# Another order on all five engines, and other PSUM banks, in a kernel of two cross-attention blocks

## The chip, the cores and the metric
The kernel runs on one core of a Trainium2 chip. The metric is the device time in microseconds (us) of one execution. Three runs of the kernel before took 1828.81, 1827.54 and 1826.35 us, median 1827.54.

## The reference, cut to what matters
x and ctx are 64 batches x 128 tokens x 256 features, float32. Two blocks follow one another; ctx is the source of keys and values in both.

```python
def block0(q, ctx):                       # 16 heads x 64
    qh, kh, vh = ln(q) @ Wq, ln(ctx) @ Wk, ln(ctx) @ Wv
    p = softmax((qh @ kh.T + rel_bias[i - j + 511]) / 8)
    x = q + (p @ vh) @ fc_w.T + fc_b
    h = ln(x)
    return x + gelu(h @ W1.T + b1) @ W2.T + b2        # 256 -> 1024 -> 256

def block1(x, ctx):                       # 16 query heads x 16, one kv head
    q, k, v = x @ Wq + bq, ctx @ Wk + bk, ctx @ Wv + bv
    p = softmax(where(window, q @ k.T / 4, -1e9))
    a = (p @ v) @ Wo + bo
    g = silu(concat(a, x) @ Wg + bg)
    o = a * g + x * (1 - g)
    y = o * rsqrt(mean(o * o) + 1e-6) * rms_w
    return y - mean(y, axis=tokens)
```

## The kernel before, in words
Two batches make a group (`GROUP = 2`), so there are `NG` = 32 groups of 256 tokens. Heads are worked on in quads: group g has four quads Q of four heads in block 0, and in block 1 two batches b of 16 heads. A number is kept as a high part (HI) and the rest (LO), and every large product is three matmuls, LO x HI, HI x LO and HI x HI: `mm3` (L616 to L618), or, where the low part comes from VectorE later than the high part from ScalarE, as two parts, `moving_hi` (L622, L623) and `moving_lo` (L626), or `standing_hi` (L630, L631) and `standing_lo` (L634). Operations that end in `_lo` are the second parts.

TensorE's operations, with the tiles into which they divide the array:
- full array, "weight-stationary": `proj_q`, `proj_k` (12 matmuls of 256 columns for one quad), `mlp_in`, `proj_q1`. The weights are the stationary operand and the tokens stream (a row names them as out<-moving,stationary: `bank<-xT,wq`). "Token-stationary" are `proj_v`, `fc`, `mlp_out`, `out_mm`, where the operands have exchanged roles (`wv,cT`, `wfc,OT`, `w,hidS`, `wog,o1T`).
- full array, others: `turn_h`, `turn_x2` (transposes, L640), `center_out` (L965, L967), which subtracts the mean over tokens.
- 64 rows: `scores(g, Q)` (L790), 16 matmuls in pairs that run side by side in the two halves of the array, into two banks.
- 64 columns: `pv(g, Q)` (L803), probabilities times values.
- 32 rows: `scores1(g, b)` (L915), 16 matmuls into four banks. 32 columns: `pv1(g, b, n)` (L928) and `kv` (L702).

The other engines empty the banks and work on what is in them. VectorE (DVE): `k_out` (L1626), `min0` and `min1` (bias or window added and row minimum, L1646, L1754), `inv`, `turn0`/`turn1` (32x32 transposes, L239), the low parts `o_lo` (L1672), `hid_lo` (L1717), layer-norm statistics. ScalarE (ACT): `exps0` and `exps1` (L2520, L2600), `q_out`, `v_out`, `hid_out`, `gelu`, the high parts `hid_hi` (L2571), `o1_hi` (L2613), `x_hat_hi` (L2636). GpSimd (POOL): `norm0`, `norm1` (L3049, L3058; probabilities times the reciprocal of their sum), the gate and residual arithmetic. SyncE (SP) issues the DMAs: `spread0`, `spread1` put the transposed probabilities where pv and pv1 read them, `keys_in` loads block 1's keys, `in_x`, `raw_x`, `out_x` and the like move activations.

Each engine has a program of its own, in an order that is written out by hand: a prologue, a loop `for r in range(3, NG - 3)` of 26 rounds (SP L519, PE L1118, DVE L2045, ACT L2764, POOL L3245), and a tail for the last groups. An engine does its list strictly in that order. A round r works on several groups at once: scores(r, ...) for group r, fc and mlp for r-1, block 1 for r-2 and r-3, proj_q(r + 1, 0) ahead. Order among engines is by semaphores that count events: `till.wait_ge("k_out", 4 * g + Q + 1)` waits until that many `k_out` were done, and the tuples in the calls, such as `("min1", 8 * r - 15)`, name the event that made the PSUM bank free (`freed`, L196). There are 8 PSUM banks; some are taken in turns through `ring_a`, `ring_c`, `ring_d`. `keep_busy` (L643) issues small matmuls that nobody reads, at four places where TensorE waits in prologue and tail.

TensorE's round before, where | is a change of tile shape (17 in a round, the last one to the next round's pv):

```
pv(r-1,2) | fc(r-1,1) k(r,0) k_lo(r,0) fc_lo(r-1,1) q(r,1) k(r,1) fc(r-1,2) | scores(r,0) | pv(r-1,3) |
scores(r,1) | fc(r-1,3) fc_lo(r-1,2) q(r,2) k(r,2) v(r,0) fc_lo(r-1,3) | scores1(r-2,1) | pv1 kv pv1 |
q(r,3) center_out(r-3,1) k(r,3) out_mm(r-2,0) out_mm_lo | pv(r,0) | scores(r,2) | turn_h v(r,1) mlp_in 0
mlp_in_lo mlp_in 1 v(r,2) mlp_in 2 fc(r,0) q(r+1,0) mlp_in 3 mlp_out(0,0) fc_lo(r,0) mlp_out(0,1)
mlp_out_lo(0,0) | pv(r,1) | scores(r,3) | pv1 pv1 | mlp_out_lo(0,1) mlp_out(1,0) center_out(r-2,0)
mlp_out(1,1) mlp_out_lo(1,0) mlp_out_lo(1,1) out_mm(r-2,1) turn_x2 q_lo(r+1) out_mm_lo q1(r-1) q1_lo
v(r,3) | scores1(r-1,0) |
```

## Time and profile before

| | before |
|---|---|
| runs | 1828.81, 1827.54, 1826.35 us |
| the profiled execution's own time | 1826.95 us |
| its span, first to last instruction | 1825.2 us |
| granted TensorE clock, mean | 0.997 of full |
| PE, PEld busy | 1792.8, 1650.3 us |
| DVE, ACT, POOL busy | 1485.3, 1535.3, 1292.3 us |

PE is TensorE's matmuls, PEld its weight loads, which lie beside them. "Busy" joins overlapping instructions; a share is of the span. Matmuls are pipelined: one is listed with 0.28 us and the next starts 0.11 us later, so distances from start to start are what adds up.

### The profile page before, as it was taken

The page shows a single profiled execution, that of the slowest core. Times are in us where ns is not written, and L with a number is a line of the kernel's source. Part 1 is how long each engine was busy: PE and PEld are TensorE (multiplying, and loading weights), DVE is VectorE, ACT ScalarE, POOL GpSimd, SP SyncE. Part 2 cuts the span into 40 slices and gives each one's busy share as a digit, 9 for nine tenths or more (in the row PEclk, how much of TensorE's full clock was granted, in tenths as well). Part 3 has the DMA queues.
Part 4 walks back from the last instruction along what each step waited for, and adds up shares of the span by engine and source line. Part 5 has one row for each costly group of instructions (what it writes and reads, how often), then busy time and mean ns, then how long its engine had stood idle before and what let it go on. Part 6 is the DMA issues. An engine that isn't in the chain of part 4 may idle for free.

```text
span 1825.2 us, 55273 instructions
## 1 busy us (share of the span) xinstructions
PE 1792.8 (98%) x18702; PEld 1650.3 (90%) x18702; DVE 1485.3 (81%) x6755; ACT 1535.3 (84%) x5586; POOL 1292.3 (71%) x1324
## 2 busy tenths in 40 slices
...
GB/s 235 124 95 116 126 122 127 122 113 114 128 118 131 121 113 114 126 119 131 121 114 114 123 121 128 121 118 112 123 124 124 121 121 112 119 118 122 103 89 59
DMA packets 238059, 219.11 MB, mean 120 GB/s; under 512 B 48848, under 2 KB 220240, under 8 KB 237776
## 3 DMA queue, kind: packets, MB, share of 16 engines
...
q14 instruction: 134, 1.10, 0.2%
...
## 4 chain that ended last, share of the span: by engine, by line
PE 90%; DVE 4%; ACT 2%; POOL 1%; DMA 1%; issue 1%; SPq 0%; POOLq 0%; DVEq 0%; ACTq 0%
PE bank L616 11%; PE bank L618 11%; PE bank L617 11%; PE bank L630 9%; PE bank L634 8%; PE bank L631 8%; PE bank L790 7%; PE bank L803 7%; PE bank L915 4%; PE bank L928 3%; PE bank L626 3%; PE bank L622 3%; PE bank L623 3%; PE bank L640 2%; DVE soft L1754 1%
## 5 line engine op out<-in xcount | busy, mean ns | idle before, releaser
L2600 ACT ACTIVATE soft<-soft,row_min 128x128 f32<-128x128 f32 x1024 | 397.3, 392 | 60.9 <-DVE row_min L1754 60.8
L2520 ACT ACTIVATE soft<-soft,row_min 128x128 f32<-128x128 f32 x1024 | 398.5, 393 | 17.1 <-DVE row_min L1646 16.6
L3049 POOL TENSOR_TENSOR soft<-soft,inv_sum 128x512 f32<-128x512 f32 x256 | 271.4, 1061 | 145.7 <-DVE inv_sum L1654 145.7
L239 DVE STREAM_TRANSPOSE turned<-soft 128x512 f32<-128x512 f32 x512 | 341.8, 689 | 10.8 <-POOL soft L3058 4.7
L3058 POOL TENSOR_TENSOR soft<-soft,inv_sum 128x512 f32<-128x512 f32 x256 | 263.9, 1042 | 60.8 <-DVE inv_sum L1763 60.7
L1754 DVE CUSTOM_DVE_ANT_0 soft<-bank,winb 128x128 f32<-128x128 f32 x1024 | 230.3, 283 | 39.0 <-PE bank L915 36.3
L1646 DVE CUSTOM_DVE_ANT_0 soft<-bank,relb 128x128 f32<-128x128 f32 x1024 | 230.0, 281 | 15.3 <-PE bank L803 5.5
L2600 ACT ACTIVATION_READ_ACCUMULATOR soft<-soft,row_min 128x1 f32 x1024 | 195.2, 191 | 0.0
L2520 ACT ACTIVATION_READ_ACCUMULATOR soft<-soft,row_min 128x1 f32 x1024 | 195.0, 190 | 0.0
L790 PE MATMUL bank<-kT,qT 64*128 64x128 f32 x2048 | 148.7, 285 | 0.7 <-DVE kT L1626 0.7
L616 PE MATMUL bank<-wv,cT 128*128 128x256 f32 x512 | 146.5, 286 | 0.0
L790 PEld LDWEIGHTS bank<-kT,qT 64*128 64x128 f32 x2048 | 124.3, 187 | 22.3 <-issue 17.2
L617 PE MATMUL bank<-wv,cT 128*128 128x256 f32 x512 | 143.4, 280 | 0.0
L618 PE MATMUL bank<-wv,cT 128*128 128x256 f32 x512 | 143.3, 280 | 0.0
L803 PE MATMUL bank<-soft,V 128*64 128x128 f32 x2048 | 140.0, 279 | 1.4 <-DMA soft<-turned 0.9
L1717 DVE TENSOR_TENSOR hidS<-hid,hidS 128x1024 fp32r<-128x1024 f32 x64 | 86.8, 1356 | 64.5 <-ACT hidS L2571 63.2
L803 PEld LDWEIGHTS bank<-soft,V 128*64 128x64 f32 x2048 | 109.2, 136 | 30.0 <-issue 19.8
L630 PE MATMUL bank<-wfc,OT 128*128 128x256 f32 x512 | 130.5, 290 | 0.0
L630 PE MATMUL bank<-w,hidS 128*128 128x256 f32 x512 | 128.0, 285 | 0.4 <-ACT hidS L2571 0.3
L631 PE MATMUL bank<-w,hidS 128*128 128x256 f32 x512 | 124.8, 278 | 0.0
L631 PE MATMUL bank<-wfc,OT 128*128 128x256 f32 x512 | 124.0, 278 | 0.0
L2552 ACT ACTIVATE hid<-bank,cols 128x256 f32<-128x256 f32 x256 | 102.3, 468 | 10.4 <-DVE hidS L1717 10.2
...
## 6 DMA issues: line engine op xcount, KB each, us to landing
soft<-turned SPq DMA_DIRECT2D x1024, 128.0 KB, 2.7
...
```

Source lines behind the costliest of these rows:

```text
L239: return eng.transpose(turned[:, slot, :, s % 2, :, :].rearrange("p j h b -> p h j b"), soft[:, s, :, :].rearrange("p h (j a) -> p h j a", ...
L616: pe.matmul(out, stat(LO), mov(HI), start=first, stop=False, **kw)
L617: pe.matmul(out, stat(HI), mov(LO), start=False, stop=False, **kw)
L618: return pe.matmul(out, stat(HI), mov(HI), start=False, stop=last, **kw)
L630: pe.matmul(out, stat(HI), mov(LO), start=first, stop=False, skip_group_check=True)
L631: return pe.matmul(out, stat(HI), mov(HI), start=False, stop=False, skip_group_check=True)
L790: last = pe.matmul(bank[i][:, h * SEQ:(h + 1) * SEQ], qT[half, Q % NQ_BUF, c, b * SEQ:(b + 1) * SEQ], kT[half, Q % NQ_BUF, c, b * SEQ:(b + ...
L803: last = pe.matmul(bank[row:row + HS, col:col + SEQ], V[:, Q % NQ_BUF, b, c * P + row:c * P + row + HS], pair_of_slots(Q % 2)[:, :, slot, ...
L2520: last = act.activation(soft[:, s, h, :], soft[:, s, h, :], ACT.Exp, bias=row_min[:, s, h:h + 1], scale=-1.0, accum_out=row_sum[:, s, h:h ...
L2600: last = act.activation(soft[:, s, h, :], soft[:, s, h, :], ACT.Exp, bias=row_min[:, s, h:h + 1], scale=-1.0, accum_out=row_sum[:, s, h:h ...
L3049: pool.tensor_tensor(soft[:, m % NS0, :, :], soft[:, m % NS0, :, :], inv_sum[:, m % NS0, :].unsqueeze(2).broadcast_to([P, QUAD, SEQ]), ALU ...
L3058: pool.tensor_tensor(soft[:, s, :, :], soft[:, s, :, :], inv_sum[:, s, :].unsqueeze(2).broadcast_to([P, QUAD, SEQ]), ALU.mult).then_inc(se ...
```

## The change
Only orders, banks and the waits that go with them are changed; the operations, their number and their inner code are the same on every engine. The rings become `ring_a` = banks (5, 6), `ring_b` = (3, 1), `ring_c` = (0, 2), and banks 4 and 7 are named alone. TensorE's round is now (15 changes of tile shape):

```
pv(r-1,2) | fc(r-1,1) v(r,0) fc_lo(r-1,1) fc(r-1,2) k(r,0) k_lo(r,0) q(r,1) k(r,1) fc_lo(r-1,2) |
scores(r,0) scores(r,1) | pv(r-1,3) | v(r,1) fc(r-1,3) fc_lo(r-1,3) q(r,2) q(r,3) | scores1(r-2,1) |
pv1 pv1 kv | k(r,2) center_out(r-3,1) k(r,3) turn_h | pv(r,0) | scores(r,2) scores(r,3) | out_mm(r-2,0)
out_mm_lo mlp_in 0 mlp_in_lo mlp_in 1 mlp_in 2 mlp_in 3 fc(r,0) q(r+1,0) v(r,2) mlp_out(0,0)
mlp_out_lo(0,0) mlp_out(0,1) mlp_out_lo(0,1) | pv(r,1) | pv1 pv1 | mlp_out(1,0) center_out(r-2,0)
mlp_out(1,1) mlp_out_lo(1,0) mlp_out_lo(1,1) out_mm(r-2,1) turn_x2 q_lo(r+1) out_mm_lo q1(r-1)
fc_lo(r,0) q1_lo v(r,3) | scores1(r-1,0) |
```

In the tail the changes of tile shape go from 82 to 72, and `keep_busy` has 7, 23, 47, 6 and 28 matmuls at five places where it had 7, 22, 44 and 12 at four. In the prologue only waits and banks at its end differ. Some waits are added that hold in round 3 only. VectorE's list puts `turn1(r-1, 0, 1)` directly ahead of `k_out(r, 1)` and three of `o_lo` at other places; GpSimd's keeps `times_z` and `minus_x` ahead of `norm1(r-2, 0, 0)` and `(0, 1)` and moves `times_gate` behind them. The diff, cut to its core:

```diff
-        ring_a = [banks[i] for i in (0, 5)]
-        ring_c = [banks[i] for i in (2, 7, 3)]
-        ring_d = [banks[i] for i in (4, 6)]
+        ring_a = [banks[i] for i in (5, 6)]
+        ring_b = [banks[i] for i in (3, 1)]
+        ring_c = [banks[i] for i in (0, 2)]
...
@@ SP, the loop
                 spread1(r - 2, 0, 1)
+                spread0(r, 0)
                 out_x(r + 1)
-                spread0(r, 0)
+                in_x(r + 1)
                 raw_x(r + 1)
-                in_x(r + 1)
                 store(r - 3, 1)
-                keys_in(r - 1)
+                tokens_c(r + 1)
                 spread0(r, 1)
-                tokens_c(r + 1)
                 spread1(r - 2, 1, 0)
                 spread1(r - 2, 1, 1)
                 out_c(r + 1)
+                in_c(r + 1)
+                keys_in(r - 1)
                 raw_c(r + 1)
-                in_c(r + 1)
+                store(r - 2, 0)
                 spread0(r, 2)
-                store(r - 2, 0)
...
@@ PE, the loop
-                proj_k(r, 1, ring_c[(r + 1) % 3], ("min1", 8 * r - 14))
-                fc(r - 1, 2, ring_a[(r + 1) % 2])
-                scores(r, 0, (ring_c[r % 3], ring_d[(r + 1) % 2]), (("min1", 8 * r - 13),), (("min1", 8 * r - 12),))
-                pv(r - 1, 3, ring_a[r % 2], ("k_out", 4 * r + 1))
-                scores(r, 1, (ring_d[r % 2], ring_c[(r + 2) % 3]), (("o_lo", 4 * r - 1),), (("v_out", 4 * r),))
...
+                proj_k(r, 1, banks[7], ("min1", 8 * r - 13))
+                fc_lo(r - 1, 2, ring_c[(r + 1) % 2])
+                if r == 3:
+                    till.wait_ge("min1", 12)
+                scores(r, 0, (banks[4], ring_a[r % 2]), (("min1", 8 * r - 12),), (("o_lo", 4 * r - 1),))
+                scores(r, 1, (ring_b[r % 2], ring_c[r % 2]), (("k_out", 4 * r + 1),), (("q_out", 4 * r + 2),))
...
+                pv(r - 1, 3, ring_b[(r + 1) % 2], ("v_out", 4 * r))
+                proj_v(r, 1, ring_a[(r + 1) % 2], ("v_out", 4 * r + 1))
+                fc(r - 1, 3, ring_c[(r + 1) % 2])
...
+                scores(r, 2, (ring_b[(r + 1) % 2], banks[4]), (("min1", 8 * r - 9),), (("y_out", 2 * r - 4),))
+                scores(r, 3, (banks[7], ring_a[r % 2]), (("k_out", 4 * r + 3),), (("k_out", 4 * r + 4),))
+                out_mm(r - 2, 0, ring_c[r % 2], ("min1", 8 * r - 8))
...
@@ ACT, the loop
                 gelu(r - 1, 1)
+                hid_hi(r - 1, 1)
                 x_hat_hi(r - 2, 0)
-                hid_hi(r - 1, 1)
+                v_out(r, 2, ring_b[(r + 1) % 2])
+                o1_hi(r - 2, 1, banks[4])
                 exps0(r, 6)
-                o1_hi(r - 2, 1, banks[1])
...
```

## Rows read from the trace of the kernel before

**Rows 1.** The page: busy us, share, instructions; shares of the last chain.
```profile
PE 1792.8 (98%) x18702; PEld 1650.3 (90%) x18702; DVE 1485.3 (81%) x6755; ACT 1535.3 (84%) x5586; POOL 1292.3 (71%) x1324
...
PE 90%; DVE 4%; ACT 2%; POOL 1%; DMA 1%; issue 1%; SPq 0%; POOLq 0%; DVEq 0%; ACTq 0%
```

**Rows 2.** One round: stretch, us, busy PE PEld DVE ACT POOL, PEclk, DMA, GB/s.
```profile
873.37:927.95 54.58, 54.56 (x580) 50.49 (x576) 45.49 (x210) 47.36 (x175) 40.32 (x42) 1.00 0.48 120
```

**Rows 3.** PE's waits from 160 to 1620 us: total, times, longest.
```profile
PE bank L790 <- DVE kT L1626: 0.7, 2, 0.5
PE bank L630 <- ACT hidS L2571: 0.3, 1, 0.3
```

**Rows 4.** Timeline of PE (start, us): scores(17, 0), pv(16, 3), scores(17, 1).
```profile
935.70 1.16 PE L790 MATMUL bank<-kT,qT 64*128 64x128 f32 x16
936.79 1.09 PE L803 MATMUL bank<-soft,V 128*64 128x128 f32 x16
937.81 0.38 PE L790 MATMUL bank<-kT,qT 64*128 64x128 f32 x2
```

**Rows 5.** Timeline of PE inside scores(17, 0): two narrow windows.
```profile
935.91 0.50 PE L790 MATMUL bank<-kT,qT 64*128 64x128 f32 x6
...
936.25 0.50 PE L790 MATMUL bank<-kT,qT 64*128 64x128 f32 x6
```

**Rows 6.** Timeline of PE: proj_k(16, 2), proj_v(16, 0), proj_q(17, 3).
```profile
887.15 0.28 PE L616 MATMUL bank<-cT,wk 128*128 128x256 f32 x1
...
888.51 0.28 PE L616 MATMUL bank<-wv,cT 128*128 128x256 f32 x1
...
888.98 0.28 PE L617 MATMUL bank<-wv,cT 128*128 128x256 f32 x1
...
947.38 0.38 PE L616 MATMUL bank<-xT,wq 128*128 128x256 f32 x1
947.61 0.28 PE L617 MATMUL bank<-xT,wq 128*128 128x256 f32 x1
...
948.78 0.28 PE L618 MATMUL bank<-xT,wq 128*128 128x256 f32 x1
```

**Rows 7.** Timeline of PE: mlp_out(15, 1, 0), out_mm(14, 1).
```profile
916.85 0.74 PE L634 MATMUL bank<-w,hidS 128*128 128x256 f32 x4
917.60 0.38 PE L630 MATMUL bank<-w,hidS 128*128 128x256 f32 x1
917.82 0.28 PE L631 MATMUL bank<-w,hidS 128*128 128x256 f32 x1
...
919.79 1.10 PE L634 MATMUL bank<-w,hidS 128*128 128x256 f32 x8
920.91 0.47 PE L630 MATMUL bank<-wog,o1T 128*128 128x512 f32 x1
921.22 0.40 PE L631 MATMUL bank<-wog,o1T 128*128 128x512 f32 x1
```

**Rows 8.** Timeline of ACT: x_hat_hi, hid_hi, o1_hi (in brackets: idle before, releaser).
```profile
916.19 0.41 ACT L2636 CAST o1T<-ag 128x256 fp32r<-128x256 f32 x1 [1.42 <-DVE ag L1810]
916.50 1.04 ACT L2571 CAST hidS<-hid 128x1024 fp32r<-128x1024 f32 x1
...
920.41 0.35 ACT L2613 CAST o1T<-bank 128x256 fp32r<-128x256 f32 x1
```

**Rows 9.** Timelines: PE scores1; DVE k_out, o_lo, k_out; POOL norm1.
```profile
926.88 1.15 PE L915 MATMUL bank<-kpar,q1T 32*128 32x256 f32 x16
...
932.59 0.84 DVE L1626 TENSOR_SCALAR kT<-bank,bk 128x256 f32<-128x256 f32 x2
...
934.57 0.65 DVE L1672 TENSOR_TENSOR OT<-bank,OT 128x512 fp32r<-128x512 f32 x1
...
935.95 0.84 DVE L1626 TENSOR_SCALAR kT<-bank,bk 128x256 f32<-128x256 f32 x2
...
932.75 1.04 POOL L3058 TENSOR_TENSOR soft<-soft,inv_sum 128x512 f32<-128x512 f32 x1 [0.35 <-DVE inv_sum L1763]
```

More of the change, by code:

```diff
@@ new lines, in tensor_program @@
+                fc(r - 1, 3, ring_c[(r + 1) % 2])
+                fc_lo(r - 1, 3, ring_c[(r + 1) % 2])
+                proj_q(r, 2, banks[7], ("k_out", 4 * r + 2))
+                proj_q(r, 3, banks[4], ("min0", 8 * r + 1))
+                scores1(r - 2, 1, (ring_a[r % 2], ring_b[r % 2], ring_b[(r + 1) % 2], ring_c[r % 2]), (("min0", 8 * r + 2),), (("min0", 8 * r + 3),), (("o_lo", 4 * r),), (("min0", 8 * r + 4),))
+                pv1(r - 2, 0, 0, ring_a[(r + 1) % 2], ("v_out", 4 * r + 2))
@@ L1350, in tensor_program @@
-            scores(NG - 1, 3, (banks[6], banks[5]), (("o_lo", 4 * NG - 3),), (("hid_out", 4 * NG - 6),))
-            mlp_in(NG - 2, 3, banks[2], ("v_out", 4 * NG - 2))
-            mlp_out(NG - 2, 0, 0, banks[7], ("k_out", 4 * NG))
+            pv1(NG - 5, 0, 1, banks[2])
+            proj_v(NG - 3, 2, banks[7], ("v_out", 4 * NG - 10))
+            center_out(NG - 6, 1, banks[4], ("min1", 8 * NG - 35))
+            proj_q(NG - 3, 2, banks[6], ("min1", 8 * NG - 34))
+            proj_q(NG - 3, 3, banks[5], ("min1", 8 * NG - 33))
@@ new lines, in tensor_program @@
+            proj_k(NG - 3, 3, banks[0], ("min0", 8 * NG - 18))
+            mlp_in(NG - 4, 2, banks[4], ("y_out", 2 * NG - 10))
+            mlp_in(NG - 4, 3, banks[5], ("ag", 2 * NG - 9))
+            scores(NG - 3, 3, (banks[2], banks[3]), (("hid_out", 4 * NG - 15),), (("hid_out", 4 * NG - 14),))
+            pv(NG - 3, 1, banks[0], ("k_out", 4 * NG - 8))
+            mlp_out(NG - 4, 0, 0, banks[6], ("o_lo", 4 * NG - 11))
+            mlp_out_lo(NG - 4, 0, 0, banks[6])
+            fc(NG - 3, 0, banks[4], ("hid_out", 4 * NG - 13))
@@ new lines, in tensor_program @@
+            pv1(NG - 4, 0, 0, banks[1], ("v_out", 4 * NG - 7))
+            pv1(NG - 4, 0, 1, banks[1])
+            kv(NG - 2, banks[2], ("o_lo", 4 * NG - 8))
+            center_out(NG - 5, 1, banks[5], ("k_out", 4 * NG - 5))
+            proj_q(NG - 2, 3, banks[4], ("x1", NG - 2))
+            out_mm(NG - 4, 0, banks[6], ("min1", 8 * NG - 27))
+            proj_v(NG - 2, 1, banks[1], ("o1_lo", 2 * NG - 7))
+            out_mm_lo(NG - 4, 0, banks[6])
+            turn_h(NG - 3, banks[0], ("min1", 8 * NG - 26))
```

1402 lines of the change are left out of this document (684 added, 718 removed).

## The prediction
> **What bounds the kernel now.** I read the page first, by engine and by chain: TensorE (PE) is busy for 1792.8 us of the 1825.2 us span and holds 90% of the chain that ended last; the other engines are busy for 71 to 84% [rows 1]. One round of the loop, from pv(r-1, 2) to the next, takes 54.58 us; PE is busy in 54.56 of them at the full granted clock (1.00) [rows 2]. From 160 to 1620 us the view of waits knows only two things that PE waited for, 1.0 us in all [rows 3]. So PE is bound by its own stream, and only what makes that stream shorter, or tears a hole in it, counts. The other four engines count where PE's cover over them gets thin.
>
> A round has some 576 matmuls, and the change neither adds nor removes one. So I took a round apart by the distance from start to start: (1) what a change of tile shape costs, (2) how far apart two like matmuls start, (3) short waits too small for the view of waits. The sum below is made against the profiled execution (1826.95 us, span 1825.2), 0.6 below the median 1827.54; at the end 0.6 is added.
>
> **1. Tile changes, 17 to 15 a round.** scores(r, 0) takes 936.79 - 935.70 = 1.09 us, from its start to that of the next block [rows 4]. It is eight pairs of matmuls, and inside such a block three pairs take 936.25 - 935.91 = 0.34 us, 0.113 a pair [rows 5]. Eight pairs are 0.91, so 0.18 us is what going into 64-row tiles and out again costs. The change puts scores(r, 0) and scores(r, 1) side by side, and scores(r, 2) and scores(r, 3): two such costs fall away, -0.37 us a round. Nothing else on PE lies beside this, it is start to start. Two of the blocks that remain now have a full-array product behind them in another place, and turn_h (128-column transposes, a cheaper start) no longer opens a stretch; for such differences I add 0.02. **-0.35 a round**, bounds -0.30 and -0.40.
>
> **2. Spacing of full-array matmuls.** The same three products start 0.113 us apart in one place and 0.118 in another. proj_k(r, 2) in the stretch that fc opens: 888.51 - 887.15 = 1.36 us for 12, 0.1133 each; from there proj_v (the operand roles exchanged) takes 0.47 for 4, 0.1175 [rows 6]. proj_q(r, 3), the first after pv1, pays 0.23 for its first step (0.11 extra, the cost of the change) and then 948.78 - 947.61 = 1.17 for 10, 0.117 [rows 6]. Reading all rounds' stretches so: after a tile change, a stretch that begins with a token-stationary product (fc, proj_v) settles to 0.113 and the weight-stationary ones behind it keep that; one that begins weight-stationary stays at 0.117 to 0.118; a step from weight- to token-stationary falls back. About half of the some 350 such distances of a round are long, 0.0046 each, 0.8 us. The new order puts proj_v(r, 1) and fc(r-1, 3) ahead of proj_q(r, 2) and (r, 3) and takes proj_v(r, 0) up behind fc(r-1, 1); but proj_k(r, 2), behind kv, still opens a stretch and out_mm opens one with mlp_in and all of mlp_in's 48 matmuls behind it. Counting so, 125 to 175 stay long, which is 0.58 to 0.80 in place of 0.81. I take **-0.12**; bounds: nearly all short -0.5, all long +0.8.
>
> The row shows two distances. The Trainium skill ("TensorE: Matmul & The Clock Gate", section "Back-to-back issue gap") gives the isolated gap at full clock as N/2.4 + 2.5 ns whatever stands before, 109 ns for 256 columns; by that the order cannot matter, this term is zero and the whole forecast 3 us higher.
>
> **3. Short waits.** Two per round. (a) mlp_out(r-1, 1, 0) needs hid_hi(r-1, 1) of ScalarE. mlp_out_lo's four matmuls ahead of it take 917.60 - 916.85 = 0.75, where 4 x 0.118 and 0.11 for the tile change are 0.58; then its first step takes 0.22 in place of 0.113: 0.17 + 0.11 = 0.28 [rows 7]. On ScalarE x_hat_hi stood ahead of hid_hi and waited 1.42 for VectorE; hid_hi ended at 917.54 [rows 8]. The change turns the two round, and mlp_out(r-1, 1, 0) now comes directly after pv1 after fc(r, 0), proj_q(r + 1, 0), proj_v(r, 2) and the first half of mlp_out. Between the end of mlp_in(r-1, 3) and it lay 24 + 4 long matmuls, pv, scores and pv1 (3.3 + 1.0 + 1.1 + 1.0, some 6.6 us with the wait); now 52 matmuls, pv and pv1, 6.0 + 1.0 + 1.0 = 8.0. ScalarE has 1.4 us more and 1.4 less to wait for. **-0.28.** (b) out_mm(r-2, 1) needs o1_hi(r-2, 1), which stood behind exps0(r, 6), at 920.41 [rows 8]. mlp_out_lo's eight take 920.91 - 919.79 = 1.12 in place of 0.94, and out_mm's first step 0.31 in place of 0.23: 0.26 [rows 7]. After, o1_hi stands ahead of exps0(r, 6), but between pv1 and out_mm lie 26 matmuls (3.1 us) where 34 and the wait lay (4.1), and x_hat_hi and v_out(r, 2) stand before it. From 0 to -0.26; I take **0**, as covers grown thin elsewhere will cost about as much.
>
> **New waits, k_out above all.** All five orders are rewritten; what each issues stays the same. The place where least is left is scores(r, 1). It needs k_out(r, 1), and that needs proj_k(r, 1). Before, fc(r-1, 2), scores(r, 0) and pv(r-1, 3) lay between the two, 8 x 0.118 + 0.1 + 1.09 + 1.02 = 3.15 us up to scores(r, 1)'s start at 937.81; k_out came at 935.95 and took 0.84 [rows 4, 9]. After, only fc_lo(r-1, 2) and scores(r, 0) lie between, 0.45 + 0.1 + 1.0 = 1.55 us. Is VectorE there in time? From scores1's start, PE needs (by its own distances) 1.07 + 1.02 + 1.0 + 1.4 + 0.47 + 0.94 + 0.91 + 0.45 = 7.3 us to the end of proj_k_lo(r, 0), 2.8 more than before, and 2.7 to the end of proj_k(r, 1), at 10.0. VectorE came to k_out(r, 0) 5.7 us after scores1's start before [rows 9]; with o_lo(r, 1) and o_lo(r, 2) now ahead (0.65 each [rows 9]) at 7.0, so it is PE that sets 7.3. From there k_out, inv, turn, moments, var, turn are some 2.4 us (3.36 before [rows 9]): 9.7, ahead of PE's 10.0. k_out(r, 1) is done at 10.9, scores(r, 1) starts at 11.5. Cover left: 0.65 us, so **0**; were it gone, each us of lateness is one of PE.
>
> The other thin covers: hid_lo(r-1, 0) must be done when mlp_out_lo(r-1, 0, 0) starts, 8 matmuls (0.9 us) behind mlp_out(r-1, 0, 0)'s start instead of 20 (2.3 us); proj_v(r, 2) is put ahead of both, 12 matmuls or 1.4 us, which gives it back. Bounds 0 to +0.3, in (b)'s allowance. On SP, spread0(r, 0) goes ahead of out_x, raw_x behind in_x, and keys_in(r-1) from behind store(r-3, 1) to behind in_c: past tokens_c, spread0(r, 1), two spread1, out_c; its data are for scores1(r-1, 0), the round's last block, some 8 us later. Queue and PE's last block leave cover, so 0; if gone, at most the 3 us of one landing a round, which I hold for unlikely. POOL, busy for 40.3 of 54.6 us [rows 2], changes only what stands before what: 0, unless VectorE waits for it (rival C). The `if r == 3` waits run once: 0.
>
> **Tail.** 82 tile changes become 72; 10 x 0.18 = 1.8, some under waits and under keep_busy's filling (85 small matmuls become 104, in places where PE waits anyway): **-1.5**, bounds -4 and +2.
>
> **Sum.** A round: -0.35 - 0.12 - 0.28 + 0 = -0.75. Times 26 rounds = -19.5; tail -1.5: -21.0. 1826.95 - 21.0 = 1805.95, plus 0.6 to the median: **1806.5 us**, -1.15%.
>
> **Rivals.**
> A, only the tile changes pay. For: every row of rows 7 is a small wait that a new small one can replace, and the spacing is a state whose cause I don't know. Against: ScalarE's x_hat_hi no longer stands in front. 26 x -0.35 - 1.5 = -10.6: 1817.
> B, the spacing becomes short nearly everywhere (-0.5 in place of -0.12): -1.13 x 26 - 1.5 = -30.9: 1797. For: "token-stationary first" in most stretches; against: out_mm and proj_k(r, 2) still open two.
> C, slower: scores(r, 1) waits for k_out(r, 1) in every round. turn1(r-2, 0, 1) now stands directly ahead of it on VectorE and needs GpSimd's norm1(r-2, 0, 1), 1.04 us, which waited 0.35 for VectorE's reciprocal and ended at 933.79 [rows 9]. If two such products come late one behind the other, VectorE is 2.1 us late, PE waits 2.1 - 0.65 = 1.45: net +0.70 a round, 26 x 0.70 - 1.5 = +16.7: 1844. It decides from 1.4 us of lateness (0.65 cover + 0.75 gain). Against: VectorE comes 0.3 us before PE by the count above, and POOL is idle for a quarter of the round. Beside this rival stands the Trainium skill ("TensorEngine Tiling (Array Packing)", section "PSUM Bottleneck"): tiling speeds TensorE up, not the emptying of PSUM, so the copy may become the bottleneck. Four score banks filled in a row are such a case; whether it binds, the waits of L790 will show.
> D, the spacing turns long everywhere (+0.8): 26 x (+0.17) - 1.5 = +2.9: 1830.5, no change.
>
> **How the numbers follow.** Forecast 0.58, A 0.20, B 0.10, C 0.07, D 0.05. The measurement can tell 0.2%, 3.7 us: faster is below 1823.9, slower above 1831.2. Faster 0.58 + 0.20 + 0.10, less 0.02 of A's edge = 0.86; same 0.06; slower 0.08. The forecast's own range, from its bounds (out_mm's wait gone, -6.8; the thin covers +0.3 a round, +7.8) is 1799 to 1814. For 8 in 10: down to 1795, which takes B's middle in, up to 1821, which takes A with a little of a thin cover; outside stay C, D and B's end.
>
> **What would show it.** The round (pv(r-1, 2) to the next) at 53.8 us; the two merged score blocks at 2.0 us each for 32 matmuls; mlp_out(r-1, 1, 0) with no long first step and ScalarE's hid_hi ahead of x_hat_hi; proj_q(r, 2) and (r, 3) at 0.113. PE's waits from 160 to 1620 us still under 3 us. It is wrong if L790 shows waits for VectorE's L1626 in most rounds (C), or if rounds stay above 54.3 us.

## The result and the profile after

The changed kernel takes 1849.04 us (median of 4 runs, 1846.52 to 1849.86), the one before 1826.94 beside it: ratio 1.0116, 95% interval 1.0103 to 1.0129. It is slower by 1.2%, where 1806.5 was forecast. The profiled execution took 1846.52 us (span 1844.7).

The page of the changed kernel, to be laid beside [rows 1]:

```profile
PE 1798.1 (97%) x18754; PEld 1666.5 (90%) x18754; DVE 1514.7 (82%) x6755; ACT 1538.9 (83%) x5586; POOL 1302.2 (71%) x1324
...
PE 60%; ACT 14%; DVE 10%; POOL 7%; DMA 4%; issue 3%; SPq 1%; POOLq 0%; ACTq 0%; DVEq 0%
```


TensorE's matmuls are busy for about as long as before, but TensorE holds only 60% of the chain that ended last (90% before); ScalarE, VectorE, GpSimd and the DMAs share the rest. The kernel has stopped being bound by one stream.

The view of windows for three rounds, columns as in [rows 2]:

```profile
442.39:498.99 56.60, 54.83 (x581) 50.84 (x577) 45.62 (x210) 47.48 (x174) 40.98 (x42) 1.00 0.48 115
940.29:995.82 55.53, 54.86 (x581) 51.20 (x577) 47.22 (x210) 47.49 (x174) 40.04 (x42) 1.00 0.48 119
1274.61:1329.14 54.53, 54.45 (x581) 50.93 (x577) 46.50 (x210) 47.59 (x174) 41.02 (x42) 1.00 0.48 120
```


Before, a round took 54.57 us to within 0.01 in most rounds. Now rounds differ: 54.5 to 56.6, mean 55.37. The best rounds are as long as one of before. The waits from 160 to 1620 us, of TensorE (to be laid beside [rows 3]), then of VectorE, then of GpSimd:

```profile
PE bank L967 <- POOL o1T L3161: 6.3, 21, 0.5
PE bank L634 <- DVE hidS L1715: 3.1, 10, 0.6
PE bank L630 <- ACT hidS L2569: 2.1, 5, 0.6
```

```profile
DVE turned L239 <- POOL soft L3056: 35.5, 81, 2.6
DVE turned L239 <- POOL soft L3047: 16.3, 20, 1.0
DVE turned L239 <- DMA soft<-turned: 8.3, 9, 1.5
```

```profile
POOL raw L3064 <- DMA raw<-in_x_t: 23.6, 26, 2.8
```


The same view of the kernel before has one line for VectorE's transposes and none for that transfer:

```profile
DVE turned L239 <- POOL soft L3058: 0.7, 3, 0.3
```


So VectorE stands for 60 us at its transposes where it stood for 0.7, most of it because GpSimd's products are late; GpSimd stands 23.6 for a transfer that it never waited for. What these lead to is seen where two rounds are laid side by side. The one from 940.29 (55.53 us), in timelines of GpSimd, VectorE, ScalarE and TensorE (in brackets idle time before it and what ended that, the releaser):

```profile
967.97 1.30 POOL L3064 TENSOR_TENSOR raw<-raw,tokens 128x512 f32<-128x512 f32 x1 [0.26 <-DMA raw<-in_x_t]
...
970.60 3.04 POOL L3056 TENSOR_TENSOR soft<-soft,inv_sum 128x512 f32<-128x512 f32 x3
...
977.96 1.30 POOL L3102 TENSOR_TENSOR xT<-raw,xT 128x512 fp32r<-128x512 f32 x1
...
984.56 1.46 POOL L3161 TENSOR_TENSOR o1T<-ag,o1T 128x256 fp32r<-128x256 f32 x1 [1.70 <-ACT o1T L2634]
```

```profile
978.25 2.10 DVE L1715 TENSOR_TENSOR hidS<-hid,hidS 128x1024 fp32r<-128x1024 f32 x1 [1.48 <-ACT hidS L2569]
```

```profile
980.44 1.57 ACT L2550 ACTIVATE hid<-bank,cols 128x256 f32<-128x256 f32 x4 [1.82 <-DVE hidS L1715]
...
983.13 1.05 ACT L2569 CAST hidS<-hid 128x1024 fp32r<-128x1024 f32 x1
984.08 0.40 ACT L2634 CAST o1T<-ag 128x256 fp32r<-128x256 f32 x1
...
986.56 0.37 ACT L2611 CAST o1T<-bank 128x256 fp32r<-128x256 f32 x1 [1.59 <-PE bank L967]
```

```profile
985.56 0.28 PE L965 MATMUL bank<-o1T,center 128*128 128x256 f32 x1
986.08 0.39 PE L967 MATMUL bank<-o1T,center 128*128 128x256 f32 x1 [0.24 <-POOL o1T L3161]
```


And the one from 1274.61 (54.53 us), VectorE and GpSimd:

```profile
1312.42 1.23 DVE L1715 TENSOR_TENSOR hidS<-hid,hidS 128x1024 fp32r<-128x1024 f32 x1 [1.10 <-ACT hidS L2569]
```

```profile
1312.53 2.28 POOL L3102 TENSOR_TENSOR xT<-raw,xT 128x512 fp32r<-128x512 f32 x1
```


GpSimd's x_lo(r+1) (L3102; the new list has it directly behind plus_x) and VectorE's hid_lo(r-1, 0) (L1715) want to run at the same time, and whichever starts first keeps its 1.30 or 1.23 us while the other is drawn out: x_lo runs from 977.96 to 979.26, and hid_lo from 978.25 takes 2.10; or hid_lo runs from 1312.42, and x_lo takes 2.28. Where hid_lo loses, the chain behind it is late: ScalarE's hid_out(2) (L2550) stands 1.82 for it, because it writes the buffer that hid_lo reads. Then follow gelu, hid_hi(1) (L2569), x_hat_hi (L2634) and GpSimd's x_hat_lo (L3161, to 986.02). TensorE's second center matmul (L967) starts 0.52 after the first, where 0.12 is usual, and ScalarE's o1_hi (L2611), whose buffer center_out reads, waits 1.59.

Over the first 25 rounds hid_lo(0) takes 1.19 to 2.33 us; rounds with over 1.8 are 55.70 on average. Those with under 1.3 are 54.97, and that average mixes two kinds, for hid_out(2) can be late by another way. In the longest round, from 442.39 (56.60 us), hid_lo is not drawn out (timelines of VectorE and ScalarE, then ScalarE's wait from 160 to 1620 us, of which the view before has none):

```profile
480.58 1.19 DVE L1715 TENSOR_TENSOR hidS<-hid,hidS 128x1024 fp32r<-128x1024 f32 x1
```

```profile
483.22 0.42 ACT L2628 ACTIVATE gate<-ag 128x256 f32<-128x256 f32 x1 [3.08 <-POOL ag L3155]
```

```profile
ACT gate L2628 <- POOL ag L3155: 15.3, 14, 3.1
```


This is square(r-2, 0), which reads what GpSimd's plus_x writes (L3155). ScalarE's new list has it ahead of hid_out(2); before, it stood behind hid_out(3). GpSimd is late with plus_x, and hid_out(2) behind square is late with it. Of the 26 rounds, five have 1.9 to 3.1 us there and hid_lo(0) at 1.19 to 1.46: they are 55.96 us on average. Ten have hid_lo(0) over 1.9: 55.70. Six have some of both: 55.03. Five have neither: 54.55. The start of hid_out(2), counted from the start of the round, and the length of the round correlate at 0.999; the duration of hid_lo(0) alone and the length at 0.41.

Before, x_lo met x_hat instead (L1810), in every round; these are the rows of that meeting (GpSimd, VectorE), ahead of the 1.42 us for which ScalarE stood in [rows 8]:

```profile
914.61 1.26 POOL L3104 TENSOR_TENSOR xT<-raw,xT 128x512 fp32r<-128x512 f32 x1
```

```profile
914.68 1.48 DVE L1810 SCALAR_TENSOR_TENSOR ag<-ag,rrms,rows 128x256 f32<-128x256 f32 x1
```


After, x_hat takes 0.48. TensorE did not feel the old meeting beyond the 0.28 of step 3a. A second meeting is new in every round: GpSimd's x_hat_lo(r-2, 0) takes 1.47 us where it took 0.73, since hid_lo(1) now runs beside it (984.56 above). Even in the best rounds center_out waits 0.2.

The Trainium skill has this rule ("SBUF — State Buffer", section "SBUF: two separate sides"): VectorE with two inputs in SBUF and a GpSimd instruction that reads SBUF share a pair of ports as an exclusive lock; whichever starts first has it for the whole instruction. The trace agrees in who loses and nearly in how much: 2.10 = 1.01 until x_lo ended + 1.09, and 2.28 = 1.12 until hid_lo ended + 1.16, where 1.23 and 1.30 are the durations without a meeting.

Start to start, a mean round of the loop divides as follows (us):

| term | before | after | forecast of the difference |
|---|---|---|---|
| matmuls at 0.1133, transposes | 39.49 | 39.49 | 0 |
| tile changes and tiled blocks, without waits | 13.75 | 13.36 | -0.35 |
| long spacing of full-array matmuls | 0.81 | 1.05 | -0.12 |
| waits, in the rows and below them | 0.58 | 1.44 | -0.28 |
| round | 54.63 | 55.37 | -0.75 |

The terms after add up to 55.34; 0.03 is left over. Of the waits after, center_out(r-2, 0) has 0.50, mlp_out(r-1, 0, 0) with its low part 0.27, scores1(r-1, 0) 0.17, the pair scores(r, 0), (r, 1) 0.12. The tail, up to the start of TensorE's last matmul, takes 238.2 us, 238.6 before: -0.4 for -1.5.

### The profile page after: what moved, and what is told of

Its sections match the earlier page's. It is cut to its first block, busy times and chain, and to the rows that moved or that the text cites. A ratio compares the mean times of both kernels' runs of the same rounds, so it can differ in the third digit from the quotient of the medians.

```text
span 1844.7 us, 55402 instructions
## 1 busy us (share of the span) xinstructions
PE 1798.1 (97%) x18754; PEld 1666.5 (90%) x18754; DVE 1514.7 (82%) x6755; ACT 1538.9 (83%) x5586; POOL 1302.2 (71%) x1324
## 4 chain that ended last, share of the span: by engine, by line
PE 60%; ACT 14%; DVE 10%; POOL 7%; DMA 4%; issue 3%; SPq 1%; POOLq 0%; ACTq 0%; DVEq 0%
PE bank L616 7%; PE bank L618 7%; PE bank L617 7%; PE bank L634 6%; PE bank L630 6%; PE bank L631 5%; PE bank L790 5%; PE bank L803 4%; PE bank L915 3%; ACT soft L2598 3%; PE bank L626 3%; ACT hid L2550 3%; PE bank L622 2%; PE bank L623 2%; ACT hidS L2569 2%
## 5 line engine op out<-in xcount | busy, mean ns | idle before, releaser
L239 DVE STREAM_TRANSPOSE turned<-soft 128x512 f32<-128x512 f32 x512 | 357.2, 701 | 71.6 <-POOL soft L3056 37.4
L790 PE MATMUL bank<-kT,qT 64*128 64x128 f32 x2048 | 137.6, 281 | 0.4 <-DVE kT L1624 0.3
L1715 DVE TENSOR_TENSOR hidS<-hid,hidS 128x1024 fp32r<-128x1024 f32 x64 | 92.2, 1441 | 52.1 <-ACT hidS L2569 51.8
L790 PEld LDWEIGHTS bank<-kT,qT 64*128 64x128 f32 x2048 | 121.8, 187 | 13.8 <-issue 7.2
L2550 ACT ACTIVATE hid<-bank,cols 128x256 f32<-128x256 f32 x256 | 102.9, 472 | 32.4 <-DVE hidS L1715 29.2
```

The costliest lines, as they stand in the source:

```text
L239: return eng.transpose(turned[:, slot, :, s % 2, :, :].rearrange("p j h b -> p h j b"), soft[:, s, :, :].rearrange("p h (j a) -> p h j a", ...
L790: last = pe.matmul(bank[i][:, h * SEQ:(h + 1) * SEQ], qT[half, Q % NQ_BUF, c, b * SEQ:(b + 1) * SEQ], kT[half, Q % NQ_BUF, c, b * SEQ:(b + ...
```

## The experiments

Each ran beside the kernel before, whose median there is 1826.8 to 1827.8; a ratio is to that. The changed kernel's 1849.04 (ratio 1.0116) is from the measurement above; differences from it are differences of medians. "Round" is the mean of the loop's 26 rounds in the profiled execution.

**1. SyncE's queue.** raw_x(r+1) was issued 20.2 us into a round before and 24.6 after, behind spread0(r, 0), out_x and in_x (which now waits for out_x to land). Timelines of SyncE, before and after (L332 out_x, L320 raw_x; the rounds start at 982.82 and 885.41):

```profile
996.55 0.59 SPq L332 DMA_DIRECT2D stats_by_row<-stat_rows  x1
...
1003.06 0.53 SPq L320 DMA_DIRECT2D raw<-in_x_t  x1
```

```profile
907.27 0.59 SPq L332 DMA_DIRECT2D stats_by_row<-stat_rows  x1
...
909.98 0.38 SPq L320 DMA_DIRECT2D raw<-in_x_t  x1
```


```diff
 # SP, loop of the changed kernel
+                out_x(r + 1)
                 spread0(r, 0)
-                out_x(r + 1)
-                in_x(r + 1)
                 raw_x(r + 1)
+                in_x(r + 1)
```

> The changed kernel with two moves on SyncE's loop alone: out_x(r+1) goes back ahead of spread0(r, 0), raw_x(r+1) back ahead of in_x(r+1). Theory Q (queue): raw_x is issued 24.6 us into a round where it was 20.2 before, GpSimd stands 23.6 us (26 times) for raw<-in_x_t, its norm1 products come late, VectorE stands 60 us at its transposes (4.8 before) and hid_lo and x_hat come late for TensorE. Then here GpSimd's wait for raw<-in_x_t is under 3 us, VectorE's waits at L239 fall from 60 to under 20 us, and the time falls by 0.5 to 0.7 us a round: 1831 to 1836 us. Rival P (products): only idle time of GpSimd moves, the waits of TensorE at center_out and mlp_out_lo stay: 1845 to 1850 us.

Measured: 1839.53 (1837.27 to 1843.9), ratio 1.0068. GpSimd's wait for raw<-in_x_t is gone, and so is ScalarE's at square; VectorE's waits at L239 fall from 60 to 36 us, where under 20 was expected; center_out's wait stays (0.51 a round). Here hid_lo(0) takes about 1.75 us in nearly every round: x_lo now starts 0.6 ahead of it each time. The time, 9.5 us of the 22 back, is between the two ranges.

**2. ScalarE's swap back, on the changed kernel.**

```diff
+                x_hat_hi(r - 2, 0)
                 hid_hi(r - 1, 1)
-                x_hat_hi(r - 2, 0)
```

> The changed kernel with ScalarE's x_hat_hi(r-2, 0) back ahead of hid_hi(r-1, 1). Theory A (the swap is what hurts): x_hat_lo and so center_out(r-2, 0), which waits 0.5 us a round, come 1.0 us earlier: -13 us, 1836, with mlp_out(r-1, 1, 0) then waiting at most 0.1. Theory Q: GpSimd and VectorE are late for other reasons; center_out's wait shrinks, mlp_out(1, 0) waits instead, 1845 to 1851 us.

Measured: 1868.95, ratio 1.0221, worse than either theory. center_out waits no more (0.236), but mlp_out(1, 0) +0.42, turn_x2 +0.54 and scores1 +0.31 a round. ScalarE is late whichever of the two goes first: the chain is late before both.

**3. center_out later on TensorE.**

```diff
                 mlp_out(r - 1, 1, 0, ring_b[r % 2])
-                center_out(r - 2, 0, ring_b[(r + 1) % 2], ("v_out", 4 * r + 3))
...
                 mlp_out_lo(r - 1, 1, 1, ring_b[r % 2])
+                center_out(r - 2, 0, ring_b[(r + 1) % 2], ("v_out", 4 * r + 3))
```

> The changed kernel with TensorE's center_out(r-2, 0) 16 matmuls (1.9 us) later, behind mlp_out_lo(r-1, 1, 1). If the wait at center_out is one that TensorE alone pays, 0.5 us a round goes: 1836 us. If the round is set by the chain of VectorE and GpSimd (theory Q), the time turns up at another wait, hid_lo's above all: 1845 to 1849 us.

Measured: 1877.62, ratio 1.0272. Neither: o1_hi(r-2, 1) writes the buffer that center_out reads, so TensorE's order is a link of ScalarE's chain. ScalarE's wait there grows from 42.2 to 74.4 us:

```profile
ACT o1T L2611 <- PE bank L967: 74.4, 26, 3.3
```


**4. The merge alone, on the kernel before.**

```diff
 # PE, loop of the kernel before
                 scores(r, 0, ...)
-                pv(r - 1, 3, ring_a[r % 2], ("k_out", 4 * r + 1))
                 scores(r, 1, ...)
+                pv(r - 1, 3, ring_a[r % 2], ("k_out", 4 * r + 1))
```

> The kernel before with one move on TensorE: pv(r-1, 3) behind scores(r, 1), so that scores(r, 0) and (r, 1) are side by side and one tile change goes. If that is worth what the prediction says, 0.18 us a round: 26 x -0.18 = -4.7, 1822.5 us. Rival (small rival C): k_out(r, 1) ended at 936.79 and scores(r, 1) would now start at 936.70; TensorE waits 0.1 to 0.2 and starts the block anew, the gain is gone: 1826 to 1830 us, and the pair of blocks takes 2.1 to 2.3 us instead of 2.0.

Measured: 1861.36, ratio 1.0184, above both ranges. The pair takes 2.71 us, pv(r-1, 3) until fc(r-1, 3) starts 1.78 instead of 1.05: 1.3 us a round for 0.19 of gain. Waits of TensorE, in that kernel:

```profile
PE bank L630 <- ACT OT L2531: 17.8, 26, 0.7
PE bank L790 <- ACT qT L2502: 10.5, 25, 0.4
```


Not k_out, which I had examined, but ScalarE's q_out(r, 1) and o_hi(r-1, 3), which I had not.

**5. fc_lo into the wait; k_out earlier** (both on the changed kernel).

```diff
 # PE
+                fc_lo(r, 0, ring_c[r % 2])
                 mlp_out(r - 1, 1, 0, ring_b[r % 2])
...
                 proj_q1(r - 1, banks[4], ("o1_lo", 2 * r - 2))
-                fc_lo(r, 0, ring_c[r % 2])
```

> The changed kernel with TensorE's fc_lo(r, 0) (4 matmuls, 0.46 us) from behind proj_q1(r-1) to ahead of mlp_out(r-1, 1, 0). Theory H (what is late is a chain that starts with hid_hi(r-1, 0): VectorE's hid_lo(0), then ScalarE's hid_out(2), gelu, hid_hi(1), x_hat_hi, GpSimd's x_hat_lo, then center_out): TensorE does 0.46 us of work where it stood, the wait at center_out(r-2, 0) falls from 0.50 to about 0.05, 26 x -0.4 = -10: 1838 us. Rival R (the whole round is a ring among the engines and TensorE's stops are only where it shows): the wait stays, 1846 to 1850 us.

Measured: 1849.11. Rival R: center_out's wait shrinks by 0.34, proj_v(r, 3) up to scores1(r-1, 0) grows by 0.46 (for ScalarE's q1_out). The wait moved, and the time stayed.

```diff
 # DVE, at the round's seam
+                k_out(r + 1, 1, banks[7])    # and not at the next round's head
                 turn1(r - 1, 0, 1)
```

> The changed kernel with VectorE's k_out(r, 1) ahead of turn1(r-1, 0, 1), 0.7 us earlier. The merged pair scores(r, 0), scores(r, 1) takes 2.10 us on average and 1.99 at best; if k_out(r, 1) being some 0.05 late is the cause, it is 1.99 in every round: -0.11 a round, 1846 us. Rival: turn1 then comes late for pv1(r-2, 0, 0), which waits; 1849 or more.

Measured: 1851.98, ratio 1.0136. The pair is 1.985 us in every round, as expected, but proj_v(r, 1) up to fc(r-1, 3) grows from 1.50 to 1.85, for o_hi(r-1, 3). Gained, and more than that paid again: the rival.

**6. The spacing, on the kernel before.**

```diff
                 pv(r - 1, 2, ring_d[r % 2], ("ag", 2 * r - 4))
-                fc(r - 1, 1, ring_a[(r + 1) % 2])
                 proj_k(r, 0, ring_a[r % 2], ("q1_out", r - 1))
                 proj_k_lo(r, ring_a[r % 2])
+                fc(r - 1, 1, ring_a[(r + 1) % 2])
```

> The kernel before with TensorE's fc(r-1, 1) from ahead of proj_k(r, 0) to behind proj_k_lo(r, 0), so that the stretch after pv begins with a weight-stationary product. If the prediction's reading of the spacing holds, proj_k and its low part go from 0.1133 to 0.1177 (12 matmuls, +0.05 us), and fc(r-1, 1) inside the stretch may bring 0.1133 back for what follows (28 matmuls, -0.13). If the order has nothing to do with the spacing, proj_k stays at 0.1133. Time 1825 to 1830 us either way.

Measured: 1825.96, ratio 0.9996 (0.9986 to 1.0006). TensorE, proj_k, proj_k_lo, fc, fc_lo, proj_q(17, 1):

```profile
928.74 0.28 PE L623 MATMUL bank<-cT,wk 128*128 128x256 f32 x1
...
929.33 0.63 PE L626 MATMUL bank<-cT,wk 128*128 128x256 f32 x4
929.79 0.28 PE L630 MATMUL bank<-wfc,OT 128*128 128x256 f32 x1
...
930.71 0.62 PE L634 MATMUL bank<-wfc,OT 128*128 128x256 f32 x4
931.17 0.28 PE L616 MATMUL bank<-xT,wq 128*128 128x256 f32 x1
...
931.96 0.28 PE L617 MATMUL bank<-xT,wq 128*128 128x256 f32 x1
```


proj_k is at 0.118 (929.33 - 928.74 = 0.59 for 5), fc_lo and proj_q at 0.114 (931.96 - 930.71 = 1.25 for 11), where they were at 0.118 before. For this stretch the reading of the rows holds in both halves. The time shows nothing: the expected net of some 0.06 us a round is below what it can tell.

**7. The swap of ScalarE, on the kernel before.**

```diff
                 gelu(r - 1, 1)
+                hid_hi(r - 1, 1)
                 x_hat_hi(r - 2, 0)
-                hid_hi(r - 1, 1)
```

> The kernel before with ScalarE's hid_hi(r-1, 1) ahead of x_hat_hi(r-2, 0), the one swap that the prediction's step 3a credits with 0.28 us a round. In the order of before ScalarE stood 1.42 us ahead of x_hat_hi, from the end of gelu at 914.77; hid_hi (1.05) fits into that, so x_hat_hi is not later. Theory: mlp_out(r-1, 1, 0) waits no more, -0.25 to -0.28 a round, 1820 to 1821 us. Rival: x_hat_hi and center_out are late as in the changed kernel, 1828 or more.

Measured: 1816.38, ratio 0.9941 (0.9929 to 0.9954): -0.47 us a round in the profile, both waits (a) and (b) of the prediction gone; better than either range. Its ScalarE (gelu, hid_hi, x_hat_hi), against [rows 8]:

```profile
909.57 1.07 ACT L2560 ACTIVATE hid<-hid 128x1024 f32<-128x1024 f32 x1
910.67 1.05 ACT L2571 CAST hidS<-hid 128x1024 fp32r<-128x1024 f32 x1
...
912.08 0.41 ACT L2636 CAST o1T<-ag 128x256 fp32r<-128x256 f32 x1 [0.36 <-DVE ag L1810]
```


**8. Three quarters of hid_lo(0) left out, on the changed kernel.**

```diff
+                n = TOK if half == 0 and g >= 2 else HH * TOK
-                dve.tensor_tensor(flat(hidS[:, LO, :, :]), flat(hid[:]), f32(flat(hidS[:, HI, :, :])),
+                dve.tensor_tensor(flat(hidS[:, LO, :, :])[:, :n], flat(hid[:])[:, :n], ...
```

> The changed kernel with VectorE's hid_lo(r-1, 0) cut to 256 of its 1024 columns (the rest of that low part is left out), so that it takes some 0.4 us instead of 1.44. Theory H: hid_lo(0) is a link of the chain hid_hi(0), hid_lo(0), hid_out(2), gelu, hid_hi(1), x_hat_hi, x_hat_lo, center_out; everything behind it comes 1.0 us earlier, TensorE's waits at mlp_out_lo (0.28 a round) and center_out (0.50) go: -0.7 x 26 = -18, 1831 us. Rival R (this chain is only one of several of like length): part of it moves to other waits, 1840 us or more.

Measured: 1827.66, ratio 1.0001, -21.4 us, somewhat more than theory H expected. In the profile hid_lo(0) goes from 1.66 to 0.95 us on average (0.42 at best, more where it still meets x_lo) and the round from 55.37 to 54.65: as much as the link. The shorter hid_lo also takes work off VectorE in general; that share isn't told apart.

**9. The merge again, with what feeds it put earlier** (kernel before, with 6 and 7).

```diff
 # PE: as in 4 and 6.  ACT: q_out(r, 1) ahead of v_out(r - 1, 3), exps0(r, 0) ahead of o_hi(r - 1, 3)
 # DVE
+                k_out(r, 1, ring_c[(r + 1) % 3])
                 inv1(r - 2, 0, 3)
-                k_out(r, 1, ring_c[(r + 1) % 3])
```

> The kernel before with hid_hi(r-1, 1) ahead of x_hat_hi on ScalarE (1816.4 us), and in addition the merge of scores(r, 0) and (r, 1) on TensorE as in the run with that one move, now with what feeds it put earlier: on ScalarE q_out(r, 1) ahead of v_out(r-1, 3) and exps0(r, 0) ahead of o_hi(r-1, 3), on VectorE k_out(r, 1) ahead of inv1(r-2, 0, 3), and proj_k(r, 0) ahead of fc(r-1, 1). If the 1.3 us a round that the bare merge cost were its feeders and nothing else, the pair takes 1.99 us and the time is 1816.4 - 26 x 0.2 = 1811 us. Rival: q_out or o_hi is late still (each was 0.4 to 0.7 us late), 1817 to 1835 us.

Measured: 1846.21, ratio 1.0097. Above both ranges. The waits are now for ScalarE's v_out (it empties a bank that scores(r, 1) fills; 8.0 us) and still for o_hi (17.9 us).

**10. GpSimd's product ahead of x_less; both repairs.**

```diff
 # POOL, loop of the changed kernel
+                norm1(r - 2, 1, 0)
                 x_less(r + 1)
                 x_norm(r + 1)
-                norm1(r - 2, 1, 0)
```

> The changed kernel with GpSimd's norm1(r-2, 1, 0) back ahead of x_less(r+1) (which stands for raw<-in_x_t). Theory Q: one of the four products that VectorE's transposes wait for no longer stands behind that transfer; the waits at L239 fall from 60 to about 45 us, the time by 0.1 to 0.2 us a round, 1844 to 1847 us. Rival: the other three still stand behind it and end the wait: 1848 to 1850 us.

Measured: 1835.39 (1833.06 to 1838.74), ratio 1.0044: -13.6, more than expected and more than SyncE's repair. But the way there was not the expected one: VectorE's waits at L239 are 66 us, not 45. What fell is GpSimd's wait for raw<-in_x_t (gone) and ScalarE's at square (15.3 us to 4.8, none over 0.4), and hid_lo(0) takes over 1.9 us in five rounds where it did in ten.

> The changed kernel with both repairs: on SyncE out_x ahead of spread0(r, 0) and raw_x ahead of in_x (1839.5 us alone), on GpSimd norm1(r-2, 1, 0) ahead of x_less (1835.4 us alone). If the two act on the same wait (what stands behind raw<-in_x_t), they do not add up: 1831 to 1836 us, with center_out's wait of 0.3 to 0.5 us a round left over from the chain through hid_lo. If they are two causes, 1849.0 - 9.5 - 13.6 = 1826 us.

Measured: 1836.24, ratio 1.0056. One cause, not two: together they give what one does. hid_lo(0) is 1.2 to 1.4 us in 21 of 25 rounds, which are 54.66 on average, and 2.2 to 2.4 in the other four, which are 55.94. The two correlate at 0.95 here, where square waits at most 0.4. So, by the rows, GpSimd's lateness costs through square and by pushing x_lo ahead of hid_lo, and less by holding up VectorE's transposes, as theory Q had it: the waits at L239 are still 64 us, and in 22 of 25 rounds of the changed kernel hid_lo waited for ScalarE, not for them.

```diff
 # ACT, with both repairs
+                v_out(r, 2, ring_b[(r + 1) % 2])
                 hid_out(r - 1, 2, ring_c[(r + 1) % 2])
...
-                v_out(r, 2, ring_b[(r + 1) % 2])
```

> The run with both repairs and, on ScalarE, v_out(r, 2) from behind x_hat_hi to ahead of hid_out(r-1, 2), into the 1.0 to 1.5 us in which ScalarE stands for VectorE's hid_lo(r-1, 0). Theory L (the changed order took away what ScalarE did in that gap: v_out(r, 1) and q_out(r, 3) stand ahead of the MLP part now): ScalarE does 0.58 us of its work in idle time, what stands behind (o1_hi, exps0(r, 6), x2_hi, q1_out) comes 0.58 earlier: 3 to 10 us less than that run. Rival: v_out is not ready there (proj_v(r, 2) ends as mlp_out starts) and holds up hid_out: slower than that run.

Measured: 1836.85, ratio 1.005. Nothing gained: moving v_out(r, 2) into the gap isn't what the round waits for. Theory L is not borne out.

> The changed kernel with both repairs (SyncE and GpSimd, 1836.2 us) and with hid_lo(r-1, 0) cut to 256 of its 1024 columns (the rest of that low part is left out; 1827.7 us when alone). If the chain through hid_lo is what is left of the loss after the repairs, TensorE's waits at mlp_out_lo and center_out go and the time nears what the tile changes alone give: 1836.2 - 13 to 18 = 1818 to 1823 us. Rival: both act on the same lateness, and the time stays at that of the cut alone, 1826 to 1829 us.

Measured: 1823.05 (1816.15 to 1825.99, 10 runs), ratio 0.9977 (0.9967 to 0.9988): below the kernel before. Its rounds are 54.48 on average. 13.2 us less than with the repairs alone, at the edge of what was expected; it includes the work that VectorE no longer does.

**11. The changed kernel's SyncE loop on the kernel before with 7.**

```diff
 # SP, loop: as in the changed kernel (the diff ahead of the prediction).  ACT: as in 7
```

> The kernel before with hid_hi(r-1, 1) ahead of x_hat_hi (1816.4 us) and with the changed kernel's loop on SyncE. raw_x(r+1) is then issued some 4 us later in the round here too. Theory: in this kernel the order on SyncE alone costs little, since TensorE has its covers and GpSimd does one product ahead of x_less: 1816 to 1820 us. Rival: the queue's order is a cost of its own of 0.37 us a round: 1826 us.

Measured: 1835.9, ratio 1.0043, +19.5 us over the run of 7: far more than expected by either side. Here another queue place shows: store(r-2, 0), which waits for VectorE's L1816, now stands ahead of spread0(r, 2), and VectorE's transposes wait for that buffer. Waits of SyncE, then of VectorE:

```profile
SPq L443 <- DVE gate L1816: 117.2, 26, 5.4
```

```profile
DVE turned L239 <- DMA soft<-turned: 49.9, 26, 2.9
```


GpSimd waits for raw<-in_x_t here too (18.7 us), and how the 19.5 us divide between the two places was not tested. The changed kernel has the same order on SyncE and stands only 8.3 us for that buffer: what an order of one queue costs hangs on the other four.

**12. A version that beats both,** 6 and 7 together, and two further moves on it.

> The kernel before with the two moves that took nothing or gained alone: hid_hi(r-1, 1) ahead of x_hat_hi(r-2, 0) on ScalarE (1816.4 us) and proj_k(r, 0) with its low part ahead of fc(r-1, 1) on TensorE (1826.0 us; proj_q(r, 1), proj_k(r, 1) at 0.1133, net -0.06 us a round). If they add up: 1816.4 - 1.6 = 1814.8 us. If not, 1816.4 or more.

Measured: **1812.76** (1811.8 to 1815.6), ratio 0.9926 (0.9914 to 0.9939), 0.8% faster than the kernel before, with two moves (7 and 6). Most of it is 7, which alone has 0.9941. What 6 adds is not clear of noise: the two 95% intervals overlap, and the profiled round goes from 54.15 to 54.13 us. Its page and one round:

```profile
PE 1777.8 (98%) x18702; PEld 1645.3 (91%) x18702; DVE 1507.1 (83%) x6755; ACT 1537.9 (85%) x5586; POOL 1293.4 (71%) x1324
...
PE 91%; DVE 3%; ACT 2%; DMA 2%; POOL 1%; issue 1%; SPq 0%; POOLq 0%; DVEq 0%; ACTq 0%
```

```profile
920.96:975.00 54.04, 54.04 (x581) 50.36 (x577) 45.39 (x210) 47.46 (x175) 40.30 (x42) 1.00 0.49 122
```


```diff
+                proj_v(r, 0, ring_c[r % 3], ("min0", 8 * r + 1))
                 proj_q(r, 2, banks[1], ("q_out", 4 * r + 2))
                 proj_k(r, 2, ring_c[(r + 1) % 3], ("k_out", 4 * r + 2))
-                proj_v(r, 0, ring_c[r % 3], ("min0", 8 * r + 1))
```

> The same two moves and a third on TensorE: proj_v(r, 0) ahead of proj_q(r, 2) and proj_k(r, 2), so that it follows the token-stationary fc_lo(r-1, 2) and does not change the kind. By the reading of the spacing its 12 matmuls go from 0.118 to 0.1133 and q, k keep 0.1133: -0.055 us a round, 1813.4 us. Rival: q_out(r, 2) comes 1.4 us later and scores(r, 2) or the exps behind it wait: over 1818 us.

Measured: 1812.97, ratio 0.9924: proj_v(r, 0) goes from 1.415 to 1.362 as expected, a size the time can't show.

```diff
+                pv(r - 1, 3, ring_a[r % 2], ("k_out", 4 * r + 1))
                 scores(r, 0, ...)
-                pv(r - 1, 3, ring_a[r % 2], ("k_out", 4 * r + 1))
                 scores(r, 1, ...)
 # ACT: v_out(r, 3) ahead of exps1(r - 1, 0, 3).  DVE: k_out as in 9
```

> The kernel before with hid_hi ahead of x_hat_hi and proj_k(r, 0) ahead of fc(r-1, 1) (1812.8 us), and with scores(r, 0) and (r, 1) side by side in another way: pv(r-1, 3) goes ahead of the two, v_out(r-1, 3) ahead of exps1(r-2, 0, 3) on ScalarE (one softmax unit of 1.55 us earlier), k_out(r, 1) ahead of inv1(r-2, 0, 3) on VectorE. The pair keeps fc(r-1, 3) 2.0 us away from pv, q_out(r, 1) keeps its 0.7 us of cover. If the covers hold, one tile change less: -0.19 x 26 = -5, 1807.8 us. Rival: scores(r, 0) is 1.0 us later for VectorE's min0 and ScalarE's exps0, which come late for what follows: 1815 us or more.

Measured: 1821.18, ratio 0.9966, 8.4 us more than without the merge. The pair is 1.985 us in every round, -0.20; but VectorE stands 34.3 us for scores(r, 0), which comes 1.0 later, and pv1(r-2, 0, 0), proj_k(r, 3) and out_mm_lo(r-2, 0) grow by 0.18, 0.08 and 0.09 a round:

```profile
DVE soft L1646 <- PE bank L790: 34.3, 26, 1.4
```


## Why the prediction was wrong, step by step

- **Tile changes, -0.35.** Right: -0.39, start to start. The second pair (scores(r, 2), (r, 3)) takes 1.99 us in every round, from 1300.07 to 1302.06; the first 2.18 in the same round:

```profile
1284.04 2.25 PE L790 MATMUL bank<-kT,qT 64*128 64x128 f32 x32
1286.22 0.98 PE L803 MATMUL bank<-soft,V 128*64 128x128 f32 x14
```

```profile
1300.07 2.06 PE L790 MATMUL bank<-kT,qT 64*128 64x128 f32 x32
1302.06 0.50 PE L630 MATMUL bank<-wog,o1T 128*128 128x512 f32 x1
```


- **Spacing, -0.12.** This term was mis-sized, and its sign was wrong: +0.24. I counted the stretch that out_mm opens as partly long; all of its 48 matmuls of mlp_in are long (5.65 us). And the rule that fc in front makes a stretch short, which held in 6, fails in the changed kernel: the stretch that fc(r-1, 1) opens is short in 16 rounds and long in 10 (proj_q(r, 1) 1.36 or 1.41), and proj_q(r, 2) and (r, 3), forecast at 0.113, take 2.81 together in 12 rounds and 2.92 in 14.
- **Short waits, step 3a, -0.28.** This step failed: the waits in all grew by 0.86. "ScalarE has 1.4 us more and 1.4 less to wait for" took hid_hi(1)'s time as given and asked only how far TensorE had moved from it. On the old order the swap is worth 0.47 a round (7). On the new one hid_hi(1) itself comes late: v_out(r, 1) and q_out(r, 3), behind which ScalarE had hidden hid_lo(0), now stand earlier, square stands in their place and waits for GpSimd, hid_lo itself is drawn out, and x_hat_hi, put behind hid_hi, ended up on the path, with x_hat_lo behind it drawn out from 0.73 to 1.47. center_out waits 0.50 where mlp_out waited 0.28.
- **New waits, 0.** This step failed too, in "POOL changes only what stands before what: 0". The changed orders of SyncE (raw_x 4.4 us later, 1) and GpSimd (norm1 behind x_less, 10) gave 13 us of the 22, by the rows through hid_out(2), which both hid_lo and square hold up; with most of hid_lo(0) left out 21 us went (8). I had priced an operation beside another engine's as free, and followed keys_in on SyncE, not raw_x. I had followed hid_lo only to mlp_out_lo (0 to +0.3; it cost 0.27), not to hid_out(2), which waits for it too. k_out's cover was as doubtful as worked out, late in part of the rounds (0.12 a round where 0.65 of cover was claimed), but not the weak place.
- **Rival C** had the right kind (VectorE stands at a transpose for GpSimd's norm1) and the wrong place and price, and 0.07 for it, 0.08 for "slower" in all, was far too little. With five rewritten orders over covers of some tenths of a us, most single moves tried here (2 to 5, 9, and the merge in 12) lost by lateness what their own term was worth, or more.
- **Rules weighed.** The Trainium skill ("TensorE: Matmul & The Clock Gate", section "Back-to-back issue gap") gives its formula by the number of columns alone and calls it the gap of an isolated matmul, not of a stream; the prediction drew from it that the order cannot matter. Run 6 shows 0.118 and 0.114 for the same products in two orders, so the measurement decides. The Trainium skill's "TensorEngine Tiling (Array Packing)", section "PSUM Bottleneck", pointed at the emptying of score banks; TensorE's waits at L790 are 0.3 us in all in the view and 0.12 a round below it, so it hardly bound here.
- **Open:** no run moved x_lo(r+1) alone, so that its meeting with hid_lo costs what the rows say is argued from rows, the correlation and the run with most of hid_lo left out. No run moved square alone, nor x_hat_lo away from hid_lo(1), and none tested the new PSUM banks apart from the orders. With both repairs and most of hid_lo left out a round is 54.48, still some 0.6 over the 53.9 that the forecast's -0.75 makes of 54.63. Of that about 0.3 is the spacing, an estimate: 199 long distances a round in that run, 164 before, at 0.0044 each, for the -0.12 of the forecast. The rest isn't taken apart.
